# Making the node half of an update layer early: a product moved from the node stage into the routing stage, kept in DRAM and added by VectorE

## What is computed

```python
msg = silu(concat(h[src], h[dst], weight) @ mW1 + mb1)
msg = silu(layer_norm(msg) @ mW2 + mb2)
agg = segment_sum(msg, src)
y   = concat(h, agg) @ uW1 + ub1          # the update's first layer: h @ uW1[:256] + agg @ uW1[256:]
x1  = x + h + silu(y) @ uW2 + ub2
x2  = layer_norm(x1)
score = x2 @ wr + br                       # rank of each row against all others
out = x1 + x2 + [rank < K] * score * (gelu(x2 @ w1 + b1) @ w2 + b2)
```

## Time and profile before

| | us |
|---|---|
| median of 3 executions | 2110.99 (2109.5 to 2112.16) |
| the profiled execution, its own time | 2107.55 |
| its span, first to last instruction | 2105.8 |
| routing, edges, nodes (from the trace) | 0 to 396, 396 to 1823, 1823 to 2106 |
| nodes: update part, feed-forward part | 1823 to 1907, 1907 to 2091, then the last store |

### The profile page before, as it was taken

One profiled execution on the slowest core, in us unless ns is written; L12 is line 12 of the kernel. 1 busy time (PEld: TensorE's weight loads), 2 busy tenths in 40 slices (PEclk: granted clock), 3 DMA queues, 4 the chain that ended last, 5 costly groups with the idle time before them and its releaser, 6 DMA issues. The chain is left out here.

```text
span 2105.8 us, 47032 instructions
## 1 busy us (share of the span) xinstructions
PE 1828.9 (87%) x11556; PEld 1600.4 (76%) x11557; DVE 1849.6 (88%) x4642; ACT 1502.1 (71%) x3084; POOL 1443.2 (69%) x1361
## 2 busy tenths in 40 slices
PE   3545664279999999999999999999999999699996
PEld 2434553269899999989999999999989998577775
DVE  5988999569999999999999999999999999654995
ACT  2322331269999999999999999999999999423322
POOL 6566887577888888888888888888888886403000
PEclk8987896589999999999999999999999999899998
DMA  4000110344333333333333333333333335101001
GB/s 134 1 3 20 30 30 17 114 141 146 103 103 104 105 103 104 103 104 104 103 103 104 103 103 104 105 103 104 103 104 104 103 103 59 43 1 25 7 1 61
DMA packets 109823, 169.21 MB, mean 80 GB/s; under 512 B 42785, under 2 KB 79571, under 8 KB 109517
## 3 DMA queue, kind: packets, MB, share of 16 engines
q0 software_dynamic: 43168, 114.55, 21.3%
q1 hardware_dynamic: 61086, 48.90, 7.6%
q10 hardware_dynamic: 5516, 5.08, 0.8%
HBM read 156.30 MB, written 11.74 MB: 80 GB/s over the span
## 5 line engine op out<-in xcount | busy, mean ns | idle before, releaser
L955 POOL DMA_INDIRECT g_rows<-b_table,idx_ring x816 | 850.9, 1043 | 237.4 <-issue 212.2
L1091 PE MATMUL ps<-w2g,nT 128*128 128x256 f32 x3432 | 815.5, 381 | 1.2 <-ACT rec L991 1.2
L1091 PEld LDWEIGHTS ps<-w2g,nT 128*128 128x128 f32 x3432 | 621.2, 191 | 68.7 <-ACT rec L991 1.4
L998 ACT ACTIVATE normed<-act,rec 128x255 f32<-128x255 f32 x858 | 467.5, 596 | 87.9 <-DVE rec L1156 81.3
L1063 PE MATMUL psH<-a_sb,ohT 128*128 x1716 | 345.3, 324 | 42.6 <-DVE ohT L1170 38.2
L1063 PEld LDWEIGHTS psH<-a_sb,ohT 128*128 128x128 f32 x1716 | 258.0, 192 | 97.1 <-issue 74.2
L1190 DVE BATCH_NORM_STATS2 rec<-act 128x6 f32<-128x256 f32 x858 | 316.8, 409 | 1.9 <-ACT act L1012 1.9
L1196 DVE TENSOR_TENSOR low<-rec,high 128x512 fp32r<-128x512 f32 x429 | 301.7, 703 | 1.1 <-ACT high L1004 1.1
L1184 DVE TENSOR_TENSOR g_rows<-psH,g_rows 128x512 f32<-128x512 f32 x429 | 292.6, 682 | 9.3 <-DMA g_rows<-b_table,rec 7.6
L1012 ACT ACTIVATE act<-g_rows 128x512 f32<-128x512 f32 x429 | 267.5, 624 | 19.7 <-DVE g_rows L1184 19.5
L1004 ACT ACTIVATE high<-rec 128x512 fp32r<-128x512 f32 x429 | 266.6, 622 | 0.2
(11 more groups left out here) (204 smaller groups left out, 2332.1 us busy)
## 6 DMA issues: line engine op xcount, KB each, us to landing
loc_rows<-loc_d SPq DMA_DIRECT2D x143, 187.5 KB
g_rows<-b_table,idx_ring POOLq DMA_INDIRECT x816, 2.8
h_sb<-in_x SPq DMA_DIRECT2D x1, 3125.0 KB
b_table<-b_out SPq DMA_DIRECT2D x25, 125.0 KB
x_all<-in_x ACTq DMA_DIRECT2D x1, 3125.0 KB
out<-x_all SPq DMA_DIRECT2D x5, 625.0 KB
ohT<-ew_d SPq DMA_DIRECT2D x143, 9.0 KB
idx_ring<-rec SPq DMA_DIRECT2D x136, 3.0 KB
```

The costliest lines, as they stand in the source:

```text
L955: pool.indirect_dma_start(g_rows[:, j, n, :], None, b_table[:, :], bass.IndirectOffsetOnAxis(ap=which, axis=0)).then_inc(s_gather[j], 16)
L998: ins = nc.scalar.activation(normed[:, (j - 10) % 2, n, 0:D - 1], act1[:, (j - 10) % RING, n, 0:D - 1], ACT.Identity, scale=rstd_e[:, g % ...
L1091: mm = pe.matmul(ps2[:, (j - 13) % 2, n, :], nT[:, (j - 13) % 2, n, q, :], w2g[:, q, :], start=(q == 0), stop=(q == 1))
```

## The change

- A DRAM buffer `u_d` holds `h @ uW1[:256]`, turned: 128 partitions, 2 halves of the output, 3125 rows.
- Routing: SP loads all of `uW1` in the routing stage, where ACT loaded it at the start of the edge stage. PE gets `updates(b)`, four products of 125 columns, between `tables(b)` and `turn(b+1)`. ACT gets `u_rows(b)` after `ab_rows(b)`. SP stores 125 KB a block in pieces of 500 bytes. `turned` waits in addition for `updates` of two blocks earlier.
- Nodes: SP loads `u_d` into `upre` in five transfers of 640 KB, ahead of the feed-forward weights. `turn` turns only agg, `first` multiplies only the agg half. DVE adds `upre` to each output of `first` into `u1` (`preacts(g)`), ACT makes Silu in place. PE now waits for DVE's add (`s_ua`) to have a `psU` bank back, not for ACT's Silu.
- DVE's order in the update part becomes `preacts(0)`, then for each group `added(g)`, `preacts(g+1)`, `normalised(g)`.

The diff, cut to its core:

```diff
@@ routing, SP
+                sp.dma_start(wts[0][:, :, :], uW1.rearrange("(k p) n -> p k n", p=P)).then_inc(s_uw1, 16)
...
                     sp.dma_start(b_table[b * NB:(b + 1) * NB, :], b_out[:, b % 2, :]).then_inc(s_bst[b % 2], 16)
+                    sp.wait_ge(s_uo, b + 1)
+                    sp.dma_start(u_d[:, :, b * NB:(b + 1) * NB], u_out[:, b % 2, :, :]).then_inc(s_ust[b % 2], 16)
@@ routing, ACT
+                def u_rows(b):
+                    act.wait_ge(s_ux, b + 1)
+                    if b >= 2:
+                        act.wait_ge(s_ust[b % 2], 16 * (b // 2))
+                    nc.scalar.activation(u_out[:, b % 2, :, :], psX[:, 2 * P:4 * P].rearrange(
+                        "p (k n) -> p k n", k=2)[:, :, 0:NB], ACT.Copy).then_inc(s_uo, 1)
...
                         ab_rows(b)
+                        u_rows(b)
@@ routing, PE
+                def updates(b):
+                    if b == 0:
+                        pe.wait_ge(s_uw1, 16)
+                    else:
+                        pe.wait_ge(s_uo, b)
+                    for f in range(2):
+                        for q in range(2):
+                            mm = pe.matmul(psX[:, (2 + f) * P:(2 + f) * P + NB], wts[0][:, q, f * P:(f + 1) * P],
+                                           hT[:, b % 2, q, 0:NB], start=(q == 0), stop=(q == 1))
+                    mm.then_inc(s_ux, 1)
...
                         tables(b)
+                        updates(b)
@@ nodes, SP
+            for g in range(NG):
+                sp.dma_start(upre[:, :, g * GN:(g + 1) * GN], u_d[:, :, g * GN:(g + 1) * GN]).then_inc(s_up[g], 16)
@@ nodes, ACT
-                        act.wait_ge(s_u, g * 4 + o + 1)
-                        if o == 0 and g:
-                            act.wait_ge(s_y, g * GB)
-                        nc.scalar.activation(u1[:, f, CUT[n]:CUT[n + 1]], psU[o % 2][:, 0:CUT[n + 1] - CUT[n]],
+                        act.wait_ge(s_ua, g * 4 + o + 1)
+                        nc.scalar.activation(u1[:, f, CUT[n]:CUT[n + 1]], u1[:, f, CUT[n]:CUT[n + 1]],
                                              ACT.Silu, bias=ub1c[:, f:f + 1]).then_inc(s_u1, 1)
@@ nodes, PE
-                    for q in range(4):
-                        from_ = (h_sb, agg)[q // 2]
-                        mm = pe.transpose(psX[b % 2][:, q * P:q * P + NB], from_[:, b, (q % 2) * P:(q % 2 + 1) * P],
+                    for q in range(2):
+                        mm = pe.transpose(psX[b % 2][:, q * P:q * P + NB], agg[:, b, q * P:(q + 1) * P],
...
-                            pe.wait_ge(s_u1, g * 4 + o - 1)
-                        for q in range(4):
+                            pe.wait_ge(s_ua, g * 4 + o - 1)
+                        for q in range(2):
@@ nodes, DVE
+            def preacts(g):
+                dve.wait_ge(s_up[g], 16)
+                if g:
+                    dve.wait_ge(s_y, g * GB)
+                for f in range(2):
+                    for n in range(2):
+                        o = 2 * f + n
+                        dve.wait_ge(s_u, g * 4 + o + 1)
+                        V.tensor_tensor(u1[:, f, CUT[n]:CUT[n + 1]], psU[o % 2][:, 0:CUT[n + 1] - CUT[n]],
+                                        upre[:, f, g * GN + CUT[n]:g * GN + CUT[n + 1]], ALU.add).then_inc(s_ua, 1)
...
+            preacts(0)
+            for g in range(NG):
+                added(g)
+                if g + 1 < NG:
+                    preacts(g + 1)
+                normalised(g)
```

More of the change, by code:

```diff
@@ L64, in build @@
     pair_block_d = nc.dram_tensor("pair_block_d", (PG, P), I32, kind="Internal").ap()
+    u_d = nc.dram_tensor("u_d", (P, 2, NODES), F32, kind="Internal").ap()
     score_d = nc.dram_tensor("score_d", (BLOCKS, NB), F32, kind="Internal").ap()
@@ L171, in build @@
             b_out = sb("b_out", [NB, 2, D], F32)
+            u_out = sb("u_out", [P, 2, 2, NB], F32)
             w2raw = sb("w2raw", [P, 2, D], F32)
@@ L208, in build @@
             s_bo = sem("s_bo")
+            s_uw1 = sem("s_uw1")
+            s_ux = sem("s_ux")
+            s_uo = sem("s_uo")
+            s_ust = [sem("s_ust0"), sem("s_ust1")]
             s_w2g = sem("s_w2g")
@@ L293, in _ @@
                 sp.wait_ge(s_bst[1], 16 * 12)
+                sp.wait_ge(s_ust[0], 16 * 13)
+                sp.wait_ge(s_ust[1], 16 * 12)
                 for g in range(TG):
@@ L373, in turned @@
                         act.wait_ge(s_ab, b - 1)
+                        act.wait_ge(s_ux, b - 1)
                     nc.scalar.activation(hT[:, b % 2, :, 0:NB], psX[:, 0:2 * P].rearrange(
@@ L973, in _ @@
                 pool.wait_ge(s_xin, 16)
-                pool.wait_ge(s_late, 16 * 6)
+                pool.wait_ge(s_late, 16 * 5)
                 for g in range(BLOCKS // 5):
@@ L1020, in bc @@
                     return v.rearrange("(a n) -> a n", a=1)
-                todo = [(wts[0][:, :, :], uW1.rearrange("(k p) n -> p k n", p=P)),
-                        (wts[1][:, :, :], uW2.rearrange("(k p) n -> p k n", p=P)),
+                todo = [(wts[1][:, :, :], uW2.rearrange("(k p) n -> p k n", p=P)),
                         (wts[2][:, :], ub1.rearrange("(k p) -> p k", p=P)),
@@ L1214, in build, with node_phase @@
                 alloc(whole, "w2s", [P, HC, D], F32), alloc(whole, "b2b", [P, D], F32))
-        node_phase(nc, io, x_v, out_v, x_sb, h_sb, agg, identf, exph, score_d, wts)
-def node_phase(nc, io, x_v, out_v, x_sb, h_sb, agg, identf, exph, score_d, wts):
+        node_phase(nc, io, x_v, out_v, x_sb, h_sb, agg, identf, exph, score_d, u_d, wts)
+def node_phase(nc, io, x_v, out_v, x_sb, h_sb, agg, identf, exph, score_d, u_d, wts):
     w1, b1, w2, b2 = io["L0_ffn_w1"], io["L0_ffn_b1"], io["L0_ffn_w2"], io["L0_ffn_b2"]
@@ L1237, in node_phase @@
         CUT = (0, 320, GN)
-        fT = sb("fT", [P, 4, GN], F32)
+        fT = sb("fT", [P, 2, GN], F32)
+        upre = sb("upre", [P, 2, NODES], F32)
         u1 = sb("u1", [P, 2, GN], F32)
@@ L1263, in node_phase @@
         s_u = sem("s_u")
+        s_up = [sem(f"s_up{g}") for g in range(NG)]
+        s_ua = sem("s_ua")
         s_u1 = sem("s_u1")
@@ L1335, in _ @@
                     nc.scalar.activation(fT[:, :, k * NB:(k + 1) * NB],
-                                         psX[b % 2][:, :].rearrange("p (q n) -> p q n", q=4)[:, :, 0:NB],
+                                         psX[b % 2][:, 0:2 * P].rearrange("p (q n) -> p q n", q=2)[:, :, 0:NB],
                                          ACT.Copy).then_inc(s_fT, 1)
@@ L1391, in first @@
                         if g * 4 + o >= 2:
-                            pe.wait_ge(s_u1, g * 4 + o - 1)
-                        for q in range(4):
-                            mm = pe.matmul(psU[o % 2][:, 0:CUT[n + 1] - CUT[n]], uw1[:, q, f * P:(f + 1) * P],
-                                           fT[:, q, CUT[n]:CUT[n + 1]], start=(q == 0), stop=(q == 3))
+                            pe.wait_ge(s_ua, g * 4 + o - 1)
+                        for q in range(2):
+                            mm = pe.matmul(psU[o % 2][:, 0:CUT[n + 1] - CUT[n]], uw1[:, 2 + q, f * P:(f + 1) * P],
+                                           fT[:, q, CUT[n]:CUT[n + 1]], start=(q == 0), stop=(q == 1))
                         mm.then_inc(s_u, 1)
@@ L1461, in _, with added @@
             V = nc.vector
-            for g in range(NG):
+            def added(g):
                 for k in range(GB):
@@ L1467, in _, with normalised @@
                     V.tensor_tensor(x_sb[:, b, :], psY[b % 2][0:NB, 0:D], x_sb[:, b, :], ALU.add).then_inc(s_x1, 1)
+            def preacts(g):
[8 more added lines that the diff above has]
+                                        upre[:, f, g * GN + CUT[n]:g * GN + CUT[n + 1]], ALU.add).then_inc(s_ua, 1)
+            def normalised(g):
                 if g:
```

## The result

The changed kernel took 2120.89 us (median; 2119.11 to 2122.2 in 5 runs) beside 2111.83 us for the kernel before in the same session (2109.5 to 2113.25). The ratio is 1.004 with a 95% interval of 1.0027 to 1.0053: slower by 5.7 to 11.2 us, against 11.0 in the sum of the prediction and 2122 as its time. The profiled execution took 2120.89 us, with a span of 2119.1.

The account below looks back on a forecast made before the run. PE was taken to bound the update part, DVE the routing while tables are made. Update part 0.0, clock 6.4 and routing 4.6 sum to 11.0 us over 2107.55, 2118.6; as a median 2122 against 2110.99, range 2111 to 2136.

Parts of the forecast that it names:

- The bound before: Update part: PE sets the end, 15.82 us a group, busy 65.6 of 68 us; DVE has slack.
- Part 1: Update part, PE: `first` 8.42 to 4.21 us a group, transposes 3.08 to 2.21; PE does not stay the bound.
- Part 2: Update part, DVE: its lump no longer lies beside `first`; cycle 16.60 us against 15.82, whole part a draw.
- Part 3: Update part: PE's clock falls at four stops of 5.2 us, 1.6 us each, 6.4 us (bounds nothing, 13.6).
- Part 4: Load of `upre`: first 640 KB needed some 5 us after the start; 0 to 1 us, taken as 0.
- Part 5: Routing: PE's `updates` ahead of `route` make DVE wait, at blocks 0, 3 and later; 4.6 us (0.4 to 21).
- The sum: Whole kernel: 0.0 + 6.4 + 4.6 = 11.0 us slower, 2122 against 2110.99.
- That the clock holds: Rival: stops of 5 us do not slow PE; update part a draw, routing 1.0 us, 2112; chance 0.12.
- Stores that hold up the scatters: Rival, routing: 500-byte stores delay POOL's scatters, POOL becomes the bound, 12.8 us more, 2135; chance 0.12.
- Faster by an overlap: Rival, update part: PE runs `second` ahead, lump overlaps `first`; 13.2 us a group, 2099 with routing; chance 0.06.

Follow-up runs that it names:

- e9: Kernel before, with only DVE's order changed: the five statistics follow the adds one by one; 2109.57 us, ratio 1.0.
- e4: Changed kernel plus 22 PE passes that nothing reads, between the second and third block of `second`; 2114.89 us, ratio 1.0021.
- e3: Changed kernel, DVE reordered: statistics behind each add, sums ahead of the next additions, one normalised row between them; 2099.88 us, ratio 0.9946.
- e1: Routing of the changed kernel with the node stage of the kernel before; `u_d` written, not read; 2111.2 us, ratio 1.0001.
- e7: Changed kernel with `updates(b)` moved behind `route` of the even window; 2117.78 us, ratio 1.0035.
- e8: e3 with `updates(b)` moved behind `route`, as in e7; 2093.13 us, ratio 0.9924 to the kernel before.
- e10: Changed kernel with DVE's lump (statistics, rows, score) ahead of the next group's additions; 2129.18 us, ratio 1.0098.

## Where the prediction was right and where not

- **The bound before** was read rightly: PE alone. e9 shows it from the other side, since DVE's order can change there without any effect.
- **Part 1**, the saving on PE: the pieces were right (`first` 4.22 us for a forecast 4.21), and as said they did not come out of the time.
- **Part 2**, the new cycle: right in mechanism and size. 16.60 us forecast, 16.64 in e4 at full clock. The addition took 0.48 to 0.49 us (0.49), the first lump ended 29.9 us after the start (30.7). That the sums agree to 0.04 us is partly luck: in e4 the twelve passes took 2.85 and not 2.59 us (three fifths of an unbroken `second` is less than twelve passes by themselves), while the add of block 0 with its signal took 0.38 for 0.46 and the lump 8.7 for 8.8.
- **Part 3**, the clock: right in mechanism, too small in size. 1.6 us a stop was taken; the stops lost 1.6 to 2.6 us, 8.5 in all for 6.4. The wait was 5.1 us three times (forecast 5.2) and 6.4 before the last, as there is no more `first` or transposes of the update behind it. The rows I had were a lower bound ("at least 0.9 to 1.3 us there"), and I stayed close to them. That the loss follows the length of the stop is not borne out either: 5.11 us went ahead of 5.48 and of 4.44 us for the same twelve passes, 2.35 us ahead of 4.54 (e3).
- **Part 4**, the load of `upre`: nothing, as said. The first addition at 1831.19 waited for PE, not for the load.
- **Part 5**, the routing: too dear. 4.6 us was forecast, and e1 allows at most 2.5. Blocks 0 and 3 paid 1.0 and 0.9 us (4.46 and 3.90 for 3.48 and 2.97 in the earlier trace rows), where I had put 0.9 and 1.4; behind them four blocks waited 0.4 to 1.0 us, where I had put three of 1.2. The single rows vary: in e1, the same routing, blocks 0 and 3 waited 5.06 and 2.77 us. One reading was wrong without harm: the table of block 2 is waited for too, 2.72 us before and 2.71 after. The clock rose, as the prediction half said: with more work PE's window, shown below, has 0.95 for 0.90 in the earlier trace rows. That this gave back what the passes cost is not shown: e7, with as many passes behind `route`, had 0.87 in this window and yet started its node stage earlier than the changed kernel, at 1822.7 us. The window of the changed kernel:

```profile
197.00:342.00 145.00, 103.47 (x944) 90.11 (x944) 140.44 (x150) 55.83 (x162) 122.22 (x174) 0.95 0.16 48
```

- **The sum** of 11.0 us was near the 8.4 measured (ratio 1.004) by luck in part: two errors of about 2 us, the clock's priced too low and the routing's too high, had opposite signs. The clock's 8.5 us lies within its bounds; the routing's, by e1, at their lower end or under it.
- **The rivals.** That the clock holds: false. Stores that hold up the scatters: the waits came (16 in the changed kernel against 5), the price did not. The step that failed there was "with that wait in each pair POOL needs 7.30 us"; the waits fell into room that POOL had. The Trainium skill, "DMA: Bandwidth & Descriptors", section "Specifications", states that a transfer below 512 bytes is done as a read-modify-write. Here the store of 500-byte pieces landed in 2.8 to 3.1 us (medians of seven profiles) and that of 1000-byte pieces in 2.7 (one profile): the sign agrees, whether a read-modify-write is behind it no run here shows, and no time hung on it. Faster by an overlap: the order did rule it out, as said; and e3 and e8 reached this rival's size by another order. That their cycle of 12.75 us is near its 13.2 is luck: 13.2 was all of DVE's work behind itself, while e3's cycle is 7.3 us of PE and 5.4 us of DVE in turn.

## What to carry to other kernels

Work that sits beside a bounding engine is free only as long as its cover is longer than it. When you shorten the bound, ask what was hidden beside it and what stands ahead of the next handover in the in-order queue: here the same instructions gave 8 us more or 11 us less, depending on where statistics and rows stood around four small additions (e3). Take such a lump apart before, or together with, the cut. And price each new stop of PE at the stop itself plus about 2 us of slowed passes behind it, until a trace shows less, as e3's did for its stops of 1.0 us; its stop of 2.35 us already cost 1.7.

## What the runs showed of the hardware

- After stops of 5.1 to 6.4 us the clock fell, and 12 passes took 4.4 to 5.5 us for 2.85; after 2.35 us they took 4.54 (e3), after 1.0 us 2.85 (e3). After 7.5 us eight passes took 4.03 to 4.53 us for 2.27 (e10). Products that nothing reads, put into the stop, held the window at 1.00 (e4) and did not delay the next block, which still waited 0.35 us or more for DVE behind them.
- With the new products ahead of `route`, PE's granted clock between 197 and 342 us of the routing was 0.94 to 0.96 in seven profiles; in the three kernels without them it was 0.87 to 0.90. Behind `route` the same products gave 0.87 once (e7) and 0.95 once (e8).
- One more store of 125 KB a block, in pieces of 500 or of 1000 bytes, goes with 15 to 20 waits of POOL's indirect scatters for 4 to 8. It is seen in the waits and not in the time.
